# Attention of a gated block in float16 pairs with scales of their own, transposed by DMA from the third batch on, and all weights rounded on POOL

## What is computed

```python
def xattn(q, k, v, Wq, Wk, Wv, Wo, bo, g):           # q = layernorm(x), k = v = ctx
    qh, kh, vh = (einsum('bcn,oc->bon', t, W).reshape(b, 8, 64, -1) for t, W in ...)
    qh = softmax(qh, axis=-2) * 64 ** -0.5            # over the 64 of a head
    kh = softmax(kh, axis=-1)                         # over the 1024 columns
    context = einsum('bhdn,bhen->bhde', kh, vh)
    out = einsum('bhde,bhdn->bhen', context, qh).reshape(b, 512, -1)
    out = einsum('bcn,oc->bon', out, Wo) + bo
    return out / maximum(sqrt(sum(out * out, axis=1)), 1e-12) * g * sqrt(128)

def bitlinear(x, w):
    scale = mean(abs(w)); q = round(clip(w / (scale + 1e-5), -1, 1))
    return x @ (q * scale).T

x = x + tanh(g_xattn) * xattn(layernorm(x), ctx, ctx, ...)
h = layernorm(x)
x = x + tanh(g_ffn) * bitlinear(bitlinear(h, w_gate) * bitlinear(h, w_up), w_down)   # 1024 -> 2752 -> 1024
```

## Time and profile before

| | |
|---|---|
| runs | 1568.46, 1570.25, 1570.53 us, median 1570.25 |
| profiled execution | 1567.98 us, span 1566.2 us |
| PE, DVE, ACT, POOL busy | 1483.3, 940.4, 640.0, 233.0 us |
| chain that ended last | PE 88%, DVE 5%, ACT 3%, issue 2%, DMA 1% |
| moved by DMA | 129.37 MB |
| mean granted clock of PE | 0.98 |

### The profile page before, as it was taken

One profiled execution on the slowest core, in us unless ns is written; L12 is line 12 of the kernel. 1 busy time (PEld: TensorE's weight loads), 2 busy tenths in 40 slices (PEclk: granted clock), 3 DMA queues, 4 the chain that ended last, 5 costly groups with the idle time before them and its releaser, 6 DMA issues.

```text
span 1566.2 us, 25411 instructions
## 1 busy us (share of the span) xinstructions
PE 1483.3 (95%) x10550; PEld 1177.7 (75%) x10550; DVE 940.4 (60%) x1298; ACT 640.0 (41%) x987; POOL 233.0 (15%) x178
## 2 busy tenths in 40 slices
PE   3675789999999999999999999999999999999999
PEld 2564678885888669885788759886798858884884
DVE  4988898865566656555565655566565555632220
ACT  4778786652434224342334324342333424330220
POOL 0212113312111111201111120111112011110000
PEclk9986889999999999999999999999999999999999
DMA  8987685231100211011110211012010120001001
GB/s 307 334 298 273 226 303 188 96 108 61 54 8 28 68 41 55 14 41 54 42 41 15 72 50 55 2 28 81 28 55 14 43 72 23 13 1 47 22 1 41
DMA packets 40978, 129.37 MB, mean 83 GB/s; under 512 B 5088, under 2 KB 5216, under 8 KB 40864
## 3 DMA queue, kind: packets, MB, share of 16 engines
q1 hardware_dynamic: 31936, 95.24, 17.4%
q10 hardware_dynamic: 8928, 32.51, 6.5%
HBM read 110.95 MB, written 16.78 MB: 82 GB/s over the span
## 4 chain that ended last, share of the span: by engine, by line
PE 88%; DVE 5%; ACT 3%; issue 2%; DMA 1%; ACTq 0%; SPq 0%; DVEq 0%
PE ps L635 36%; PE ps L660 19%; PE ps L479 8%; PE ps L481 8%; PE ps L480 8%; PE ps L517 3%; PE ps L548 3%; PE ps L606 1%; PE ps L538 1%; PE ps L614 1%; DVE q_stat L974 1%; ACT w_gu L730 1%; DMA ct_raw<-in_ctxt 0%; DVE e_lo L831 0%; DVE absum L856 0%
## 5 line engine op out<-in xcount | busy, mean ns | idle before, releaser
L635 PE MATMUL ps<-zT,w_gu 128*128 128x256 f16 x5504 | 630.4, 273 | 0.0
L635 PEld LDWEIGHTS ps<-zT,w_gu 128*128 128x128 fp8e4 x5504 | 531.9, 98 | 80.3 <-issue 13.9
L660 PE MATMUL ps<-w_dn,inter_buf 128*128 128x512 fp8e4 x1376 | 307.9, 379 | 0.4 <-DVE inter_buf L831 0.4
L660 PEld LDWEIGHTS ps<-w_dn,inter_buf 128*128 128x128 f16 x1376 | 131.6, 98 | 156.6 <-issue 9.0
L1092 POOL TENSOR_TENSOR qs<-qs,q_stat 128x1024 f32<-128x1024 f32 x64 | 124.4, 1943 | 493.4 <-DVE q_stat L990 493.4
L1033 DVE SCALAR_TENSOR_TENSOR gate<-ps,gate 128x256 f32<-128x256 f32 (+1 forms) x176 | 73.8, 419 | 156.9 <-ACT gate L671 155.3
L671 ACT ACTIVATE gate<-ps 128x256 f32<-128x256 f32 (+1 forms) x176 | 67.0, 380 | 206.2 <-PE ps L635 205.2
L831 DVE TENSOR_TENSOR inter_buf<-gate,inter_buf 128x256 f16<-128x256 f32 (+1 forms) x176 | 84.3, 479 | 79.6 <-ACT inter_buf L671 79.4
L778 ACT ACTIVATE qs<-qs 128x1024 f32<-128x1024 f32 x64 | 67.5, 1054 | 154.7 <-DVE qs L982 154.7
L671 ACT ACTIVATE inter_buf<-gate 128x256 f16<-128x256 f32 (+1 forms) x176 | 73.1, 415 | 93.0 <-DVE gate L1033 93.0
L671 ACT ACTIVATE k_hi<-ps 128x1024 fp32r<-128x1024 f32 (+1 forms) x80 | 75.1, 938 | 83.2 <-PE ps L517 43.3
(11 more groups left out here) (115 smaller groups left out, 2145.6 us busy)
## 6 DMA issues: line engine op xcount, KB each, us to landing
inter_buf<-in_gate_w SPq DMA_DIRECT2D x20, 512.0 KB, 5.8
inter_buf<-in_up_w SPq DMA_DIRECT2D x20, 512.0 KB, 5.4
w_dn<-in_up_w SPq DMA_DIRECT2D x20, 512.0 KB, 5.3
w_dn<-in_down_w SPq DMA_DIRECT2D x20, 512.0 KB, 5.0
w_dn<-in_gate_w SPq DMA_DIRECT2D x19, 512.0 KB, 6.0
ct_raw<-in_ctxt ACTq DMA_DIRECT2D x16, 512.0 KB, 3.6
xb<-in_x ACTq DMA_DIRECT2D x16, 512.0 KB, 3.7
x_dram<-xb SPq DMA_DIRECT2D x16, 512.0 KB, 2.9
```

Source lines behind the costliest of these rows:

```text
L635: last = nc.tensor.matmul(ps[:, j % 2, s * T:s * T + T], w_gu[:, w, k, :], zT[:, h, k, :], start=(k == 0 and h == 0), stop=(k == NC - 1 an ...
L660: mm = nc.tensor.matmul(ps[:, hf, :], lhs, w_dn[:, j, hf * 512:hf * 512 + 512], start=(u == 0), stop=(u == total - 1))
```

## The change

- All attention products take float16 halves. So that the values fit, the context, the small weights and the product m are scaled by maxima of their own: DVE takes the absolute maximum of each partition (`cabs`, `mabs`, `lmax`), PE adds the 128 of them with one matmul against ones (`csum`, `msum`, `lsum`), DVE turns the sum into a scale (`cscale`, `mscale`, `lscale`). `kexp` gets a scale and a bias from them (one more DVE operation, `kbias`), `qsum` one more as well.
- From batch 2 on (`BY_PE` = 2) `ktr` and `tr` are gone. ACT and DVE split the unturned k and probabilities in SBUF (`kf_hi`, `kf_lo`, `qf_hi`, `qf_lo`), and SP issues a DMA transpose for both halves at once, 512 KB (`turn_k`, `turn_q`). The context (`turn_c`) and the FFN's input (`turn_z`) go this way in all batches, so `in_ctxt` and `zt` are gone too. `k16` and `p16`, from which they are read, exist once. `y`, `sq` and the FFN's input `z32` share one buffer.
- All 66 roundings are POOL's (`QUANT_POOL`); 11 were.
- `wload` moves from SP to ACT, the loads of x and context from ACT to SP.
- From batch 2 on the projections use PSUM's `PROJ` and `TR` pairs in turn, where they used `PROJ` alone.
- All tables of times are new.

```diff
-FFN_FROM = (1935, 3774, 5567)
-EVERY = 1792
+BY_PE = 2
+FFN_FROM = (1969, 3625, 5231)
+EVERY = 1607
...
+    "kf_hi": [[], [], [1365, 1570, 1650, 1770], [1993, 2162, 2276, 2365], [2864, 2969, 3046, 3133], [3595, 3693,
+        3781, 3878], [-773, -653, -576, -478], [-30, 68, 156, 253]],
+    "turn_k": [[], [], [1394, 1596, 1714, 1803], [2037, 2206, 2313, 2391], [2905, 2996, 3083, 3173], [3642,
+        3730, 3827, 3912], [-705, -626, -529, -440], [17, 106, 202, 287]],
+    "ctxk": [[373, 507], [1027, 1165], [1667, 1874], [2285, 2463], [3054, 3247], [3799, 3987], [-558, -378],
+        [174, 362]],
+    "qf_hi": [[], [], [1615, 1815, 1928, 2201], [2392, 2561, 2699, 2849], [3217, 3321, 3464, 3629], [4011, 4138,
+        4292, 4448], [-397, -311, -162, 4], [386, 513, 667, 823]],
+    "turn_q": [[], [], [1669, 1858, 2146, 2253], [2419, 2598, 2725, 2877], [3248, 3347, 3509, 3670], [4037,
+        4164, 4319, 4499], [-362, -285, -116, 45], [412, 539, 694, 874]],
...
-QUANT_POOL = [("wquant", m, c) for _, m, c in QUANTS + DOWN_QUANTS if m == DOWN and c % 2]
+QUANT_POOL = QUANTS + DOWN_QUANTS
...
         def proj_bank(i, n):
 
-            return 0 if i < GB and n % 2 else PROJ
...
+            return PROJ if n % 2 == 0 else 0 if i < GB else TR
...
+            def turn_c(i, _):
+                wait(sp, c_lo_s, i + 1)
+                wait(sp, ctxk_done, 2 * i)
+                sp.dma_start_transpose(cT[:, :, :, :].rearrange("p s c n -> p (s c) n"),
+                                       c16[:, i % 2, :, :].rearrange("p s n -> p (s n)")).then_inc(cT_in, 16)
+
+            def turn_k(i, p):
+                wait(sp, kf_lo_s, PAIRS * (i - BY_PE) + p + 1)
+                wait(sp, ctxk_done, 2 * i + p // 2)
+                o = (p % 2) * P
+                sp.dma_start_transpose(kT[:, :, :, o:o + P].rearrange("p s c d -> p (s c) d"),
+                                       k16[:, :, :].rearrange("p s n -> p (s n)")).then_inc(kT_in, 16)
...
+            def csum(i, _):
+                pe.wait_ge(started, 2)
+                wait(pe, c_max, i + 1)
+                wait_banks(proj_free[PROJ])
+                total(ps[:, PROJ, 0:1], cmx[:, 0:1]).then_inc(c_sum, 1)
+                proj_free[PROJ][0] = (c_ranged, i + 1)
...
+                if i < BY_PE:
+                    wait(pe, k_lo_s, PAIRS * i + 2 * h + 2)
+                else:
+                    wait(pe, kT_in, 16 * (PAIRS * (i - BY_PE) + 2 * h + 2))
...
+                    if i < BY_PE:
+                        wait(pe, e_lo_s, NU * i + 2 * hf + 2)
+                    else:
+                        wait(pe, eT_in, 16 * (NU * (i - BY_PE) + 2 * hf + 2))
...
+            def wload(m, c, n):
+                kind = STAGED[n][0]
+                s = SLOT[n]
+                if n == 0:
+                    act.wait_ge(ctx_in, 16)
+                wait_stage_done(act, BEFORE[n])
...
+            def kf_hi(i, p):
+                n = PAIRS * (i - BY_PE) + p
+                wait(act, k_exp, PAIRS * i + p + 1)
+                wait(act, kT_in, 16 * n)
+                copy(k16[:, 0, :], ek[:, p % 2, :]).then_inc(kf_hi_s, 1)
...
+            def qf_hi(i, u):
+                wait(act, q_prob, NU * i + u + 1)
+                wait(act, eT_in, 16 * (NU * (i - BY_PE) + u))
+                copy(flat(p16[:, 0, :, :]), flat(qs[:, u % 2, :, :])).then_inc(qf_hi_s, 1)
...
+            def absmax(out_ap, v):
+                return nc.vector.tensor_reduce(out_ap, v, AX_X, ALU.max, apply_absolute_value=True)
...
+            def kf_lo(i, p):
+                wait(dve, kf_hi_s, PAIRS * (i - BY_PE) + p + 1)
+                minus(k16[:, 1, :], ek[:, p % 2, :], k16[:, 0, :]).then_inc(kf_lo_s, 1)
```

More of the change, by code:

```diff
@@ L663, in down @@
                         mm.then_inc(down_ready, 1)
[L665 to L666 removed]
+            program({"prod": prod, "lsum": lsum, "csum": csum, "msum": msum, "kt": kt, "qt": qt, "tr": tr,
+                     "mprod": mprod, "ctxk": ctxk, "ktr": ktr, "wtotal": wtotal, "outp": outp, "ss": ss, "R": R,
+                     "gu": gu, "down": down})
         @block.scalar
```

644 lines of the change are left out of this document (381 added, 263 removed), and 69 rows, old and new, of tables (DOWN_AT, GU_AT, PLAN, QUANT_AT).

## The result

The changed kernel takes 1527.8 us (median of 4 runs, 1526.1 to 1532.6) against 1569.4 us for the kernel before on the same chip: a ratio of 0.9741, with a 95% interval of 0.9721 to 0.9762, so 2.6% faster. The forecast was 1446 us, 7.9% faster. The direction held and the time lies in the stated range, but the size is wrong: 82 us are missing, two thirds of the gain. The profiled execution took 1532.6 us, 4.8 more than the median.

What follows compares the result with a forecast made beforehand. PE was taken as the bound from 206 us on, no engine before. Opening 210, first group 170, five full groups 806.5, then 140.2 and 115.9 gave 1442.6 us of span, 1446 us as time; range 1420 to 1560.

Steps and rivals of the forecast that it cites:

- PE's saving: Full groups: float16 and dropped transposes, less added sums, save PE 10.1 us per batch, 20.2 per group.
- The landing: DMA transposes of 512 KB, ten per batch: taken to land in 3 to 5 us, bounds 2.9 to 8.8.
- a rival: Slower case: transposes land later than the table allows, 70 us lost per us over 5.1; chance 0.17.
- break-even 6.9: Transpose landing, in us, at which the forecast gain of 124 us would be used up.
- The two figures of the Trainium skill: Transpose landing: 261 GB/s, estimated 2.0 us for 512 KB; or 1309 ns per block, estimated 21 us for sixteen in series.
- DVE and POOL: Full groups: DVE gains about 3 us per batch, some 115 of 161 us; POOL's added roundings fall mostly in the opening.
- a bound only: Opening: DVE's relief from 44 roundings (39 us) counted only as the -10 us bound.
- up to 17 us of DVE for POOL: Whole kernel: 112 subtractions slowed by the SBUF interface shared with POOL; 0 on the path while idle time covers it.
- I take +4 us: Opening: grows from 206 to 210 us as the table does, with bounds of -10 and +30.
- as the engines are at 0.13 here: Full groups: DMA engines' busy share, given as reason for a landing nearest to plain loads, 3 to 5 us.
- 170: First group, in us: 188.4 - 20.2 = 168, and 2 for down weights rounded on one engine.
- The third rival: Opening stretches by 20 to 35 us since ACT's row blocks on loads: 1465 to 1480 us; chance 0.12.

Runs made afterwards that it cites:

- m1: DMA alone, without attention or feed-forward: 512 KB transposes or plain copies beside 0, 1, 3 or 6 weight loads; a transpose landed in 24.6 us beside six.
- e4: Changed kernel with the rounding of gate, up and half of the down weights back on DVE: 1537.4 us.
- e2: Changed kernel with all 144 DMA transposes made plain copies of the same bytes, transposition left out: 1441.3 us.
- e5: Changed kernel with the 22 transposes up to batch 3 made plain copies, transposition left out: 1445.3 us.
- e11: Changed kernel with one edit, the weight loads back on SP's queue, all transposes kept: 1459.4 us.
- e9: Changed kernel with 16 of the 22 transposes, keys and probabilities of batches 2 and 3, made plain copies: 1496.5 us.
- e7: Changed kernel with 6 of the 22 transposes, context of batches 0 to 3 and z of 0 and 1, made plain copies: 1500.8 us.
- e8: Changed kernel with weight loads back on SP's queue and x and context loads back on ACT's, all transposes kept: 1457.3 us.
- e12: Changed kernel with the transposes moved to ACT's queue, where the weight loads are: 1543.1 us.

## Why the prediction was right and wrong

**PE's saving was right.** The timeline of PE in a full group of the changed kernel (start, length, what) has `ctxk` from 827.21 to 829.83, six matmuls of `qt` from 831.58 to 832.87, and `msum`.

```profile
827.21 0.27 PE L572 MATMUL ps<-kT,cT 128*128 128x256 f16 x1
...
829.83 1.91 PE L741 MATMUL ps<-zT,w_gu 128*128 128x256 f16 x16
831.58 0.38 PE L572 MATMUL ps<-wq,qn 128*128 128x512 f16 x1
...
832.87 5.40 PE L741 MATMUL ps<-zT,w_gu 128*128 128x256 f16 x48
...
844.66 0.28 PE L589 MATMUL ps<-mmx,cst 128*128 128x1 f32 x2
844.80 0.38 PE L572 MATMUL ps<-wq,qn 128*128 128x512 f16 x1
```

So 2.62 us for 24 (forecast 2.62), 1.29 for six (1.30) and 0.14 for `msum` (0.3 taken). A full group is 161.94 us (161.3), with PE busy all through. The fp32r matmul was at nearly a column a cycle, and float16 earned only what the earlier trace rows said.

**The landing was right for the full groups, and a rival fell.** 4.5 us there (3 to 5 taken, break-even 6.9), and 4.3 alone in m1. The two figures of the Trainium skill that the prediction named miss from both sides: the 2.0 us estimated from DMA: Bandwidth & Descriptors, Latency and other measured facts, was too short (even six of them one behind the other moved 211 GB/s, from 40 to 54 us in m1), and the 21 us from VectorE: DVE Perf Modes, The three transpose paths, is not reached, so the sixteen blocks don't follow one another at that price.

**DVE and POOL were right.** `minus` on k has a median of 1218 ns with a few long ones, as feared and without effect:

```profile
L949 DVE TENSOR_TENSOR k<-ek,k x56: 1211/1218/2912, 179.1 to 1303.9; 128x1024 f16<-128x1024 f32 x56
```

DVE is busy for 113.2 us of a full group (115 forecast). The roundings are off the path, and the move earned 10 us at most (e4), which the forecast had counted as a bound only. The forecast allowed up to 17 us of DVE for POOL beside the 112 subtractions of k and the probabilities. In the trace five of them take 1.67 to 2.91 us, each while a POOL instruction runs, and that is 4.5 us above five medians of 1.22.

**The step that failed is the opening's "I take +4 us".** It asked what moving `wload` to ACT costs ACT (0.33 us an issue; rightly nothing, as e2 shows), and not what it does to the two queues. Before, no large transfer of SP's queue had to pass the weight stream, since the stream was SP's queue. The landing of 3 to 5 us was taken "as the engines are at 0.13 here", a row of a full group, and used for the 22 transposes up to batch 3 too, where the earlier trace rows has the engines at 0.82 in the opening and at 0.42 in the first group. The change puts the stream in one queue and the transposes in another; 82 us of 82 hang on these 22 transfers (e5), and 68 of them on the queue of the weight loads (e11). The same step left the first group at "170": it lasts 191.8 us, and 171.4 with its own ten of the 22 plain (e9). The third rival had the right place and the wrong cause: the opening stretched by 65 us, by no wait of ACT for its loads (e2 has the same row of ACT and opens in 206.2 us). "DMA engines idle at 0.13" was a statement on one stage, and I carried it to another. A slip of adding is beside this: 1444.4 + 2.3 is 1446.7, not 1446.

Left open: why taking away 6 of the 22 gives 27 us, the other 16 give 31, and both together 82. One thing can be read: with one half plain, transposes of the other half meet the loads that are left. In e9 the fourth `cT` and the second `zT` land in 23.4 and 20.8 us (9.0 and 5.3 in the changed kernel), in e7 the first four `kT` in 19.2 (median, 15.1 there). That this is all of it is not shown. Open too are the 12 us between e8 and plain copies (e5), which may be the transposes' larger engine time (20 transfers from 790 to 952 us, the same with plain copies 27.5% of 16 engines for SP's queue, with transposes 47.9%: 1.65 us more each).

## What to carry to other kernels

Ask of each transfer on which somebody waits what else is in flight at that time, and from which queue: many small packets beside a stream of large ones in another queue land late, in 6.0 to 24.6 us here instead of 4.3, and hold up all that stands behind them in their own. Put the stream and the urgent small-packet transfer into one queue, in the order in which they are needed, and not into the queue of an engine that computes (e12). And take the price of a transfer from the stage where it runs: the same transpose cost nothing on the path in a full group, and 22 of them cost 82 us in the opening and the first group.
